# Loading the closing part's first heads and rows during attention's last tile, with the wait for the last head stores moved to the last batch's load

## The reference

```
ffn(x)  = tanh(((x @ W) @ W1) @ W2 + bias)
attn(x) = softmax((content + relative_shift(pos)) / 4) @ v, heads joined, @ Wo + bo
          content = (q + u) @ k^T, pos = (q + v_bias) @ (pe @ Wp)^T

x = x + 0.5 * ffn(layernorm(x))
x = x + attn(layernorm(x) * g + b)
x = x + 0.5 * ffn(layernorm(x))
```

## Time and profile before

| | us |
|---|---|
| time, median of 3 runs | 3412.76 |
| the three runs | 3412.76, 3432.28, 3412.55 |
| profiled execution, its own time | 3411.35 |
| its span, first to last instruction | 3409.6 |
| mean granted TensorE clock in it | 0.991 |

### The profile page before, as it was taken

The page is one execution under the profiler, slowest core; times in us unless marked ns, Lnnn a source line. Parts: engine busy times, 40 slices in busy tenths (PEclk is TensorE's granted clock), DMA queues, the critical chain, the costliest instruction groups (busy, mean ns, idle before and its releaser), DMA issues. The chain is left out here.

```text
span 3409.6 us, 110393 instructions
## 1 busy us (share of the span) xinstructions
PE 3353.8 (98%) x34876; PEld 2084.8 (61%) x34876; DVE 1945.4 (57%) x5651; ACT 2329.6 (68%) x3255; POOL 1327.2 (39%) x1341
## 2 busy tenths in 40 slices
PE   7998999999999999999999999999999999999988
PEld 5674666666666666666666666666666666666677
DVE  7872555555555555555555555555555555555557
ACT  3344777777777777777777777777777777777633
POOL 2211444444444444444444444444444444444400
PEclk9997999999999999999999999999999999999999
DMA  5989999999999999999999999999999999999862
GB/s 166 285 255 312 399 389 390 388 388 386 391 386 389 388 390 389 387 389 387 390 386 389 389 389 388 388 390 387 387 389 390 387 388 391 388 386 389 303 200 98
DMA packets 433553, 1231.27 MB, mean 361 GB/s; under 512 B 48992, under 2 KB 133472, under 8 KB 433504
## 3 DMA queue, kind: packets, MB, share of 16 engines
q1 hardware_dynamic: 429424, 1228.07, 96.0%
q10 hardware_dynamic: 4080, 2.58, 0.3%
HBM read 617.04 MB, written 613.43 MB: 361 GB/s over the span
## 5 line engine op out<-in xcount | busy, mean ns | idle before, releaser
L894 POOL TENSOR_SCALAR at_pos_in<-at_pos_in,at_neg_max 128x1024 f32<-128x1024 f32 x1024 | 1146.0, 1119 | 1685.9 <-DVE at_neg_max L857 1685.9
L819 ACT ACTIVATE at_pos_out<-at_ps_pos 128x1024 f32<-128x1024 f32 x1019 | 1044.5, 1025 | 505.1 <-PE at_ps_pos L731 505.1
L857 DVE CUSTOM_DVE_ANT_0 at_pos_in<-at_ps_con,at_pos_in 128x512 f32<-128x512 f32 x1024 | 708.5, 692 | 1172.0 <-PE at_ps_con L731 800.3
L731 PE MATMUL at_ps_con<-keep_right,keep_left 32*128 32x512 f32 x4116 | 1338.5, 643 | 2.1 <-ACT at_pos_out L819 1.1
L828 ACT ACTIVATE at_prob<-at_ps_turn 128x512 f32<-128x512 f32 x2048 | 1111.5, 595 | 283.1 <-PE at_ps_turn L764 242.1
L731 PE MATMUL at_ps_pos<-keep_right,keep_left 32*128 32x512 f32 x4076 | 1156.1, 643 | 12.8 <-PEq L97 12.8
L764 PE MATMUL at_ps_turn<-keep_ident,at_pos_in 128*128 128x128 f32 x8192 | 1105.7, 278 | 0.0
L764 PEld LDWEIGHTS at_ps_turn<-keep_ident,at_pos_in 128*128 128x128 f32 x8192 | 890.6, 141 | 155.5 <-issue 153.3
L777 PEld LDWEIGHTS at_ps_pv<-at_prob,keep_v_aug 128*32 128x32 f32 x16384 | 385.3, 109 | 773.3 <-issue 773.2
L857 DVE CUSTOM_DVE_ANT_0 at_pos_in<-at_ps_con,at_pos_in,at_neg_half 128x512 f32<-128x512 f32 x1024 | 769.0, 751 | 135.0 <-PE at_ps_con L731 0.4
L777 PE MATMUL at_ps_pv<-at_prob,keep_v_aug 128*32 128x128 f32 x16384 | 659.2, 279 | 0.8 <-issue 0.8
(11 more groups left out here) (94 smaller groups left out, 1397.9 us busy)
## 6 DMA issues: line engine op xcount, KB each, us to landing
scratch_scores<-at_pos_out SPq DMA_DIRECT2D x1024, 512.0 KB, 10.1
at_pos_in<-scratch_scores SPq DMA_DIRECT2D x1024, 512.0 KB, 10.3
keep_left<-scratch_queries SPq DMA_DIRECT2D x127, 256.0 KB, 10.1
scratch_queries<-fr_qk SPq DMA_DIRECT2D x124, 256.0 KB, 3.9
fr_x<-in_L_attn_x_dram SPq DMA_DIRECT2D x16, 512.0 KB, 6.4
scratch_x<-fr_x_bo SPq DMA_DIRECT2D x16, 512.0 KB, 5.0
scratch_keys<-fr_qk SPq DMA_DIRECT2D x32, 256.0 KB, 5.4
scratch_values<-fr_values SPq DMA_DIRECT2D x8, 1024.0 KB, 5.8
```

The costliest lines, as they stand in the source:

```text
L731: return pe.matmul(banks[:, n, :], left[side][rows, t.i * P:(t.i + 1) * P], right[side][rows, :], start=True, stop=True)
L819: act.activation(pos_out[:, t.slot, :], banks[:, :, :].rearrange("p a m -> p (a m)"), ACT.Copy)\
L857: dve.tensor_tensor_reduce(pos_in[:, t.slot, keys], ps_con[:, n, :], pos_in[:, t.slot, keys], -SCALE, 3.0e38 if n == 0 else neg_half[:, t. ...
L894: pool.tensor_scalar(pos_in[:, t.slot, :], pos_in[:, t.slot, :], -1.0, neg_max[:, t.slot:t.slot + 1], ALU.mult, ALU.add).then_inc(shifted, 1)
```

## The change

One head buffer (`heads`), two x1 buffers (`x1_bo`) and their semaphores become the program's own, allocated before attention, so that they can be filled while attention runs; `head_out` is kept past attention too. In SyncE's list, at the first step past the last tile (`r * BODY + t == NT`), `load_ahead` waits for the first batch's head stores (8 on each side) and issues the loads of heads 0 and of x1 0 and 1. The wait for all head stores goes from attention's end to the load of the last batch's heads (`load_heads(7)`). The closing part then begins with x1 2, heads 1, x1 3, heads 2. Nothing is changed in what is computed.

```diff
@@ attention_phase, SyncE
-        head_out = sems("head_out", 2)
+        head_out = keep["head_out"]
...
+            def load_ahead():
+                for k in range(2):
+                    sp.wait_ge(head_out[k], 16 * H // 2)
+                sp.dma_start(keep["heads"][:, :, :], a["heads"].rearrange("(b h) p n -> b p h n", b=B)[0])\
+                    .then_inc(keep["heads_in"], 16)
+                for k in range(2):
+                    sp.dma_start(keep["x1_bo"][k][:, :, :], a["x1"].rearrange("(g t p) d -> p g t d", p=P, t=GROUP)[:, k, :, :])\
+                        .then_inc(keep["x1_in"][k], 16)
...
+                if isinstance(r, int) and r * BODY + t == NT:
+                    load_ahead()
...
-            for k in range(2):
-                sp.wait_ge(head_out[k], 16 * UNITS // 2)
-
@@ closing_phase
-        heads = ring(HEAD_RING, "heads", [P, H, P])
-        x1_bo, x2 = ring(X1_RING, "x1_bo", [P, GROUP, D]), ring(X2_RING, "x2", [P, GROUP, D])
+        heads = [keep["heads"]] + ring(HEAD_RING - 1, "heads", [P, H, P])
+        x1_bo, x2 = keep["x1_bo"] + ring(X1_RING - 2, "x1_bo", [P, GROUP, D]), ring(X2_RING, "x2", [P, GROUP, D])
...
             def load_heads(b):
+                if b == B - 1:
+                    for k in range(2):
+                        sp.wait_ge(keep["head_out"][k], 16 * UNITS // 2)
                 sp.dma_start(heads[b % HEAD_RING][:, :, :], head_rows[b]).then_inc(heads_in[b % HEAD_RING], 16)
...
-            for b in range(HEAD_RING):
-                load_heads(b)
-            for g in range(X1_RING):
-                load_x1(g)
+            load_x1(2)
+            load_heads(1)
+            load_x1(3)
+            load_heads(2)
@@ macaron_layer
+        keep["heads"] = sb("heads", [P, H, P])
+        keep["x1_bo"] = [sb(f"x1_bo{k}", [P, GROUP, D]) for k in range(2)]
         attention_phase(nc, keep, a)
```

More of the change, by code:

```diff
@@ L947, in closing_phase @@
                                           for n in ("head", "proj", "z", "ffn"))
-        heads_in, x1_in, out_done = sems(HEAD_RING, "heads_in"), sems(X1_RING, "x1_in"), sems(2, "out_done")
+        heads_in, x1_in = [keep["heads_in"]] + sems(HEAD_RING - 1, "heads_in"), keep["x1_in"] + sems(X1_RING - 2, "x1_in")
+        out_done = sems(2, "out_done")
         stats_ready, moments_ready, variance_ready, scale_ready, z_ready = (
@@ L1125, in macaron_layer @@
         keep |= {n: [ctx.enter_context(nc.semaphore(f"keep_{n}{k}")) for k in range(2)]
-                 for n in ("x1_out", "qk_out", "v_out", "q_in", "k_in", "vals_in")}
-        keep |= {n: ctx.enter_context(nc.semaphore("keep_" + n)) for n in ("first_in", "p_ready", "blanked")}
+                 for n in ("x1_out", "qk_out", "v_out", "q_in", "k_in", "vals_in", "head_out", "x1_in")}
+        keep |= {n: ctx.enter_context(nc.semaphore("keep_" + n)) for n in ("first_in", "p_ready", "blanked", "heads_in")}
         front_phase(nc, keep, a)
+        keep["heads"] = sb("heads", [P, H, P])
+        keep["x1_bo"] = [sb(f"x1_bo{k}", [P, GROUP, D]) for k in range(2)]
         attention_phase(nc, keep, a)
```

## The result

| | before | changed |
|---|---|---|
| time, median of 20 runs | 3412.55 us | 3403.67 us |
| profiled execution, its own time | 3411.35 us | 3404.41 us |
| its span | 3409.6 us | 3402.6 us |

The change makes the kernel faster. The ratio is 0.9966 with a 95% interval from 0.9951 to 0.9981. The medians differ by 8.9 us, the two profiled executions by 6.9 us; the interval covers both (it stands for 6.5 to 17 us). Of the 20 runs of each kernel, 17 before took 3409.80 to 3413.27 us and 19 after took 3401.85 to 3405.00; these two bands don't touch. The others, at 3430 to 3449 before and 3422 after, pull the ratio to 11.6 us, beyond what the medians show. Of the trace I use the differences inside one execution, which are much finer than that.

The account below looks back on a forecast made before the run. TensorE, busy 98%, was taken as the bound, with a 10.28 us gap at the barrier to gain from; 7.7 (earlier start) + 0.5 (clock) + 0 = 8.2 us gave 3404.6 us, range 3401 to 3408.5.

Parts of the forecast that it names:

- The loads ahead: SyncE's queue after head 126's store: three loads issued by 3240.6, heads 0 landed at 3240.7, cost 0.
- The removed wait: SyncE at attention's end: without the last store's wait, the closing part starts at 3244.77; the wait costs 0 at heads 7.
- The start of the closing part: ScalarE's first regrouping finds heads 0 there and starts at 3244.8 in place of 3252.54, 7.7 us earlier.
- The clock: TensorE's first closing instructions: half clock costs 2.9 us before and 2.4 after, a 0.5 us gain, between +2.9 and -2.4.
- The loads behind the barrier: SyncE's closing loads, x1 2 ahead of heads 1: regroup 2 hidden with 1.7 us to spare; cost 0, at most 3.
- The sum: Whole kernel: 7.7 + 0.5 + 0 = 8.2 us gain, giving a median of 3404.6 us.
- what a measurement can tell: Whole-kernel timing: 1% (34 us) is about what can be told from no change; within 1% given 0.97.
- The clock that stays up: Rival, TensorE's closing start: clock stays at 1.00 through the pauses; gain 10.6 us, time 3402.2; chance 0.2.
- Late heads: Rival, closing loads: the wait moves to heads 1 behind x1 2; gain 5.3 to 6.3, about 3407 us; chance 0.1.
- A barrier that drains the queues: Rival at the barrier: the last store is still waited for; 1.3 us back, 3405.9 us; chance 0.03.
- Code loading: Rival at the branch into the closing part: an engine waits for code not there yet; 1.6 us, 3406.2; chance 0.03.
- Attention slowed by the buffers' places: Rival in attention: buffers moved by 16 KB per partition slow its transfers; at 1% of the rate 3434 us; chance 0.04.

Follow-up runs that it names:

- the kernel before, filled: Kernel before plus 20, 56 and 14 idle identity transposes on TensorE (attention's end, closing start, between first two transpose groups): 3454.41 us, ratio 0.9992.
- the second profile: The changed kernel run again with no edit, on a later chip: 3448.14 us against 3453.94 for the kernel before, ratio 0.9975.
- the places only: Kernel before with the three buffers allocated ahead of attention, its own order of loads and waits kept: 3450.79 us, ratio 0.9993.
- the filled kernels: Kernels with idle TensorE transposes: changed kernel 3442.8 us, kernel before 3454.41, with heads 1 first 3444.42, between the first two transpose groups only 3435.88 and 3441.92.

## Why the prediction was right or wrong

**The loads ahead: right.** They were issued from 3234.67 on, ended their issue before head 127 was ready, and heads 0 was there in time. SyncE's issue cost stayed covered: attention's last TensorE instruction starts 0.26 us later than before, within what two executions differ by. Heads 0 landed 6.6 us after its issue, at 3241.3; 3240.7 was forecast. The run with the loads after the last store shows that the stretch between the two stores is what hides them.

**The removed wait: right, with its size.** Predicted 1.3 us (3246.03 to 3244.77); put back it costs 1.30 in TensorE's gap, and moved alone it brings 1.34.

**The start of the closing part: right.** Predicted 7.7 us earlier; relative to attention's end it is 9.17 - 1.33 = 7.84. The first transposes follow the last attention instruction by 2.44 us, where the sign set for it was 2.5 to 2.7.

**The clock: the mechanism right, the size wrong, and in the first profile the sign.** The step said that the clock would fall in the second pause and cost 2.4 us, so that its term would be a gain of 0.5. In the profile it fell at 3245.0, in the first pause, and cost 3.4, of which 5.12 - 3.46 = 1.66 in the product and 2 x (1.97 - 1.09) = 1.76 in the turnings; the kernel before, filled, put its price at 2.8. So the term is a loss of 0.6 in this execution. In the second profile the fall came in the second pause, as forecast, the cost was 2.5, and the term was a gain of 0.3 (11.64 - 11.34). The kernel before has such a spread too: its chain took 11.64 in its own profile and 12.05 with the places only. The forecast lay within what the same program does in different executions, but a single value for it was more than the rows could give. What sets the moment of the fall stays open. The full-clock length of the chain, 8.8, was right (8.85 and 8.84). The rule of the Trainium skill (TensorE: Matmul & The Clock Gate, "What's actually happening") that activity releases the slow clock agrees with the filled kernels, 1.00 throughout in all five of their profiles.

**The loads behind the barrier: right that they cost nothing.** The forecast had heads 1 landing at 3253.2, 8.0 us after an issue at 3245.2, and regroup 2, free from 3252, done at 3254.3; that already holds a wait of about 1.2 us, hidden with 1.7 to spare. It landed at 3254.3, 8.8 us after its issue at 3245.50, ScalarE waited 1.24 us, and 1.6 us were to spare before its transposes. In five other profiles with x1 2 alone ahead of it, heads 1 landed 7.0 to 7.5 us after its issue, so 8.8 is the slowest of six. The first product hid the wait, and issuing heads 1 first changed the stretch by 0.03 us, that is by nothing. The prediction named a gap put down to the DMA of heads as a sign of being wrong: the gap appeared and meant nothing, since its own times had that gap in them.

**The sum.** 7.7 + 0.5 = 8.2 was forecast. In the stretch after attention the two profiles differ by 7.26, and the second profile of the changed kernel is 8.15 under the one before; the medians differ by 8.9. What the medians have beyond the stretch, 0.7 to 1.6 us, no run here explains. The forecast of 3404.6 stands 0.9 us above the measured 3403.67 and inside the range.

**The step that failed: what a measurement can tell.** The prediction took 1% (34 us) for about what a measurement of this kernel can tell from no change, and put 0.97 on no difference by over 1%. The gain is indeed under 1%, but 20 runs gave an interval of 0.9951 to 0.9981 that leaves 1 out. Two of the three runs shown ahead of the prediction lay within 0.2 us of each other, with the third 19.5 us above; the text took its 1% from none of them, and should have worked out from them that a gain of 8 us, 0.24%, could well be told from none. The measured intervals are 0.15 to 0.27% to either side, four to six times finer than 1%. On the later chips 8 us is at the edge of that: the changed kernel's second interval leaves 1 out (0.9957 to 0.9992), that of heads 1 first, with the same stretch as the first profile within 0.03 us, does not (0.9958 to 1.0004). Of the terms that make up the time, the one mis-sized is the clock's: 2.4 us of cost were forecast, and 3.4 and 2.5 measured.

**The rivals.** The clock that stays up did not come by itself; it had to be made by filling, and then gave 10.7 us in the stretch, the 10.6 forecast for it. Late heads appeared as a wait and cost nothing. A barrier that drains the queues is out: the first closing load is issued at 3244.93, 0.4 us after the last store's issue ended, while that store landed 1.6 us after its issue began, at 3245.78. Code loading is out too: the changed kernel's trace has one transfer of instructions (0.02 MB) in 3240 to 3246, but it lies in 3240.0 to 3240.5, 4 us ahead of the barrier, and SyncE and ScalarE start the closing part 0.40 and 0.43 us after SyncE's last issue ended, so neither stood waiting for its code. Attention slowed by the buffers' places was not seen, within the width of that comparison.

## What to carry to other kernels

Between two parts of a program, count what SyncE waits for at the barrier and what the next part's first instruction waits for: both can go if the first load can be issued at a quiet place of the queue ahead of the last store, and the final wait can be put where it has long been met. Only the load that the first instruction needs must go ahead (heads 0, not x1). A shorter gap doesn't keep TensorE's clock up if the new part starts with short bursts; a few idle transposes in such a pause brought another 2.5 to 3.4 us in the trace here, and the kernel with the change and 14 of them has the shortest stretch (155.5 us against 166.2), in both of its profiles.

## What the runs showed of the hardware

The granted clock fell 1.4 us after attention's last TensorE instruction in the changed kernel's first profile and 4 us after it in the second, with the first turning in between. In the kernel before it was still 1.00 for 2.6 us and then fell just before 3248, 4.6 us after that instruction:

```profile
3246.00:3248.00 2.00, 0.00 (x0) 0.00 (x0) 0.00 (x0) 0.00 (x0) 0.00 (x0) 0.99 0.14 10
3248.00:3252.50 4.50, 0.00 (x0) 0.00 (x0) 0.00 (x0) 0.00 (x0) 0.00 (x0) 0.50 0.98 284
```

So the time since the last instruction alone doesn't say when. The same program's first turning took 1.97 us in one profile and 1.09 in another.

A load of 1 MB of heads with no other load ahead of it landed 6.3 to 6.8 us after its issue. With one load of 0.5 MB issued ahead of it, it landed 7.0 to 7.5 us after its issue in five profiles and 8.8 in one; the earlier load's bytes alone, at 349 GB/s, would take 1.5.
